# GpSimd starts splitting the second expert's weights after the whole table of tiles instead of after its rows

## The reference

```python
gate_logits = x @ gate_w + gate_b                       # 8 experts
weights, indices = top_k(gate_logits, 2); weights = softmax(weights)
h = einsum('bsd,edh->ebsh', x, w1) + b1                 # w1[e]: 256 x 2048
xh, gh = split(h, 2);  act = silu(gh) * xh
out_e = einsum('ebsf,efd->ebsd', act, w2) + b2          # w2[e]: 1024 x 256
out = sum of the two chosen experts' out_e * weights
x = layernorm(x + out)
```

## Time and profile before

| | us |
|---|---|
| median of 3 runs (lowest, highest) | 1397.85 (1397.28, 1399.97) |
| the profiled execution's own time | 1405.77 |
| its span, first to last instruction | 1403.8 |
| TensorE busy (matmul) | 1253.7, 89% |
| VectorE busy | 1143.5, 81% |
| ScalarE busy | 797.6, 57% |
| GpSimd busy | 786.8, 56% |
| mean granted TensorE clock | 0.959 |

### The profile page before, as it was taken

How to read it: one execution, slowest core, us unless ns; L and a number is a source line. 1 busy time by engine, 2 the same in 40 slices (tenths; PEclk the granted TensorE clock), 3 DMA queues, 4 the chain that set the end, 5 groups by cost and what they waited for, 6 DMA issues and landing times. The chain is left out here.

```text
span 1403.8 us, 40595 instructions
## 1 busy us (share of the span) xinstructions
PE 1253.7 (89%) x13192; PEld 1031.3 (73%) x13193; DVE 1143.5 (81%) x2632; ACT 797.6 (57%) x1863; POOL 786.8 (56%) x743
## 2 busy tenths in 40 slices
PE   4889999999999999899978879999999999999990
PEld 2456666666666676667667768999999999999980
DVE  4889999999999999899976886868677867686666
ACT  5666666666766766676634344544545455445446
POOL 3467676666766787687775340707043706170772
PEclk9899999999999999999966989999999999999995
DMA  6213432334443223321225542231514151412554
GB/s 211 81 35 121 135 100 85 111 109 135 136 136 106 96 62 122 108 87 58 91 112 147 141 118 58 67 117 41 146 45 138 42 146 45 137 43 56 150 144 157
DMA packets 120720, 146.63 MB, mean 104 GB/s; under 512 B 47744, under 2 KB 103552, under 8 KB 120512
## 3 DMA queue, kind: packets, MB, share of 16 engines
q1 hardware_dynamic: 109504, 102.15, 24.1%
q0 software_dynamic: 10848, 42.32, 9.7%
q10 hardware_dynamic: 288, 1.19, 0.2%
HBM read 98.83 MB, written 37.47 MB: 97 GB/s over the span
## 5 line engine op out<-in xcount | busy, mean ns | idle before, releaser
L1111 PE MATMUL pe<-arena 128*128 128x128 f16 x3408 | 218.8, 222 | 26.0 <-issue 19.1
L1111 PEld LDWEIGHTS pe<-arena 128*128 128x128 f16 x3408 | 202.5, 99 | 32.6 <-issue 30.7
L1111 PE MATMUL pa<-arena 128*128 128x128 f16 x3408 | 217.7, 221 | 3.1 <-DVE pm L2315 2.5
L1136 PE MATMUL py<-arena 128*128 (+1 forms) x1704 | 199.4, 274 | 5.5 <-issue 3.3
L1111 PEld LDWEIGHTS pa<-arena 128*128 128x128 f16 x3408 | 200.1, 99 | 3.4 <-DVE pm L2315 2.7
L1572 ACT ACTIVATE arena<-pe,arena 128x128 f32<-128x128 f32 x568 | 161.4, 370 | 68.0 <-PE pe L1111 67.5
L1705 DVE SCALAR_TENSOR_TENSOR arena<-pa,arena 128x511 f32<-128x511 f32 (+2 forms) x240 | 178.7, 745 | 11.7 <-ACT arena L1209 5.6
L1136 PEld LDWEIGHTS py<-arena 128*128 128x128 f16 x1704 | 164.5, 98 | 24.8 <-issue 5.0
L1744 DVE TENSOR_TENSOR_SCAN arena<-arena,pe 128x512 f32<-128x512 f32 x128 | 148.8, 1203 | 3.0 <-issue 1.6
L2557 POOL TENSOR_SCALAR arena<-arena 128x1536 f16<-128x1536 f32 (+2 forms) x35 | 45.3, 1295 | 180.7 <-DVE arena L2363 175.3
L833 PEld LDWEIGHTS py<-arena 128*128 128x128 f32 x1024 | 124.0, 197 | 17.4 <-issue 8.5
(11 more groups left out here) (306 smaller groups left out, 2542.1 us busy)
## 6 DMA issues: line engine op xcount, KB each, us to landing
arena<-step_rows SPq DMA_DIRECT2D x64, 512.0 KB, 5.8
arena<-in_w_exp POOLq DMA_DIRECT2D x32, 768.0 KB, 4.9
arena<-queue SPq DMA_DIRECT2D x74, 129.5 KB
answer<-arena SPq DMA_DIRECT2D x71, 128.0 KB, 1.7
arena<-in_x SPq DMA_DIRECT2D x16, 512.0 KB, 6.1
answer<-zeros SPq DMA_DIRECT2D x10, 512.0 KB, 4.8
arena<-h SPq DMA_DIRECT2D x9, 512.0 KB, 6.2
h<-arena SPq DMA_DIRECT2D x8, 512.0 KB, 3.0
```

The lines of the kernel that those rows point to most:

```text
L1111: ins = pe.matmul(bank[:, f * P:(f + 1) * P], w_split[:, p, hl, d * 2 * FF + col:d * 2 * FF + col + P], x_hl[:, r, x, d * P:(d + 1) * P], ...
L1136: ins = pe.matmul(py[:, 0:D], a[:, b, f, :], part(p, hl, W1N + f * D, D), start=(half == 0 and n == 0), stop=(half == 1 and n == len(passe ...
```

## The change

GpSimd's wait before the split of place 1 becomes the wait for `plan_done`; the separate wait for `plan_done` before the split of place 2 falls away, being the same one. Nothing else is changed: the same instructions, the same loads, the same order on every engine.

```diff
                     pool.wait_ge(w_have, 1)
                 load_weights(e)
                 if e == 1:
-                    pool.wait_ge(rows_done, 1)
-                if e == 2:
                     pool.wait_ge(plan_done, 1)
                 if e >= 2:
                     end_e = pool.value_load(plan_i[0:1, 3 * NJT + NE + e - 2:3 * NJT + NE + e - 1], min_val=0, max_val=NJ)
```

## The result

| | before | changed |
|---|---|---|
| median, us (lowest to highest) | 1399.97 (1397.27 to 1404.04), 7 runs | 1392.64 (1389.72 to 1396.23), 7 runs |
| ratio, 95% interval | | 0.9949 [0.9928, 0.9969] |
| the profiled execution's span | 1403.8 | 1392.5 |

The kernel became faster by 0.5%, 7.3 us between the medians. The forecast was 6.9 us.

A forecast was written before the change was run, and what follows sets the result against it. The prediction took TensorE as the bound, waiting early in the expert stage for VectorE held by GpSimd. -9.4 gained + 2.5 new waits = -6.9 us, so 1397.85 became 1391.0 us, range 1386.0 to 1396.5.

The forecast's parts named there:

- What bounds it, and why VectorE was slow: Expert stage: TensorE bounds; at its start GpSimd's split holds VectorE's SBUF steps, and TensorE loses 11.12 us.
- The gain, 9.4 us: TensorE from product (0,2) to (1,1): 11.12 us lost, less 1.72 kept, gives 9.4 gained.
- The part I kept, 1.72 us of start-up after plan_done: TensorE's idle after plan_done, read as fetching the table's word and new code; 1.72 us expected to stay.
- What comes, 2.5 us of new waits: VectorE held under the later split 1 makes TensorE wait up to (2,2)'s stretch: 2.5 us, bounds 0 and 9.4.
- +4.7 forecast: VectorE's rows_moved, eight chained steps under split 1: seven held, meeting four GpSimd instructions, +4.7 us.
- The held first step of rows_of_pick: VectorE under split 1: the first rows_of_pick meets at most the split's last instruction; no size added.
- Kept at their price: 4.4 us ahead of and in the product of (2,0): TensorE's 2.66 us idle before the product at 841.00 plus 1.7 of lower clock, assumed to stay.
- more gained: Rival, chance 0.13: with third-expert loads later, the stall at product (2,0) goes too; -11.3 us, 1386.6.
- split 2 was released 9.4 us earlier and not 7: Sign of being right in the changed profile: GpSimd's split 2 released 7 us earlier.
- the signs of being wrong: TensorE's VectorE waits between 811 and 835 over 5 us, lower clock past 10 us, or plan_done not 7 us earlier.
- Moved, not removed: Rival, chance 0.13: VectorE's held time under the later split reaches TensorE, up to 9.4 us; 1397 to 1398.
- Slower: Rival, chance 0.08: each held rows_moved step waits out its own GpSimd instruction; +6.2 us, 1404.

The follow-up runs named there:

- e5: Kernel before, with split 1's 15 GpSimd instructions replaced by zero fills that write SBUF and read none; 1390.04 us, ratio 0.9939.
- e0: Kernel before run once more with no edit, as a control; ratio 0.9999 [0.9981, 1.0016].
- e2: Kernel before, with the third expert's weight loads waiting until tile (2,0) is answered, split 1 unmoved; 1396.91 us against 1400.08, ratio 0.9986.
- e7: Kernel before, split 1 still from rows_done, with only VectorE's rows_moved and rows_of_pick steps put two tiles later; ratio 1.000 [0.9983, 1.0018].
- e6: Kernel before, with split 1 started after words, between rows_done and plan_done; 1391.54 us, ratio 0.9945 to the kernel before.
- e3: Changed kernel, with VectorE's rows_moved and rows_of_pick steps put two tiles later, behind split 1; 1389.97 us, ratio 0.9922 to the kernel before.
- e8: The kernel of e3 run again beside the changed kernel; 1390.18 us, ratio 0.9929 to the kernel before.

## Why the prediction was right

The forecast was -6.9 us, with a range of 1386.0 to 1396.5; measured 1392.64, and 7.3 us between the medians. Step by step:

*What bounds it, and why VectorE was slow.* Right. In e5 GpSimd keeps its 15 instructions but reads nothing, and the two-operand steps run free beneath them. The fills are shorter than the split's instructions too, but length alone does not explain it, since a copy and a cast are held beneath the same fills.

*The gain, 9.4 us.* The loss from (0,2) to (1,1) was 11.1, 8.6, 13.6 and 13.3 us in the four traces with split 1 from rows_done and its arithmetic unchanged (before, e0, e2, e7) and 0.7 in the three of the changed kernel: 10.9 us gained on the mean. The part I kept, 1.72 us of start-up after plan_done, was too dear. It is paid where TensorE already stands waiting (1.72 to 1.76 us from plan_done to the next bank in before, e0, e2, e7 and e6); with plan_done early, 0.57 remains. plan_done came at 804.3, 1.7 us ahead of the forecast. Of that, 0.7 is held time in three rows that I had left out (L2227, L2232, L2255), and 1.1 is that VectorE stood further ahead in that execution before the split began. TensorE had no use for it.

*What comes, 2.5 us of new waits.* The mechanism was right and the size low: 2.0, 3.7 and 3.9 us of waits on VectorE in three traces. Shorter delays that the view does not mark come on top. From the product of (1,1) to that of (2,2) the changed kernel lost 4.6, 6.4 and 6.6 us and e3 and e8, which do not wait for VectorE, 1.4 and 1.6. Between the means that is 4.4 us, where the medians of the two pairs give 2.8 and 3.2. Of its terms rows_moved was over-sized, +4.7 forecast and +3.2 measured (4.70 against 1.54), since it met three GpSimd instructions and not four, and only steps with two operands were held; in e6, where five of the eight steps were held, L2266 among them, it cost +3.5. The held first step of rows_of_pick, +1.9 (2.29 against 0.38), I had named and not added, and the last of the new waits (0.95) stands right behind it. e3 and e8 show the two together: without them under the split, the waits are gone.

*Kept at their price: 4.4 us ahead of and in the product of (2,0).* This was the weakest step. I took one profile's stall for the kernel's. At that product nothing was marked in e0 and e2, and 1.74 us in e7, each with matmuls at full pace behind. So it was one execution's and not the kernel's, and the rival "more gained", which took it as a whole, could only come true in the profiled pair (-11.3 us), not in the medians (-7.3). A smaller part of it may be real: the four traces with split 1 from rows_done lost 3.6 us on the mean from (1,1) to (2,2) without any wait on VectorE, and e3 and e8 lost 1.5.

*The sum.* In the traces the stretch up to (2,2) lost 15.3 us on the mean of the four with split 1 from rows_done (17.9, 11.1, 15.3, 16.7) and 6.6 in the three changed: -8.7, to be set beside -7.3, -7.3 and -6.3 between medians; so few traces can't settle the rest. By its parts it is -10.9 up to (1,1), +4.4 from VectorE's lateness behind it and -2.2 from start-up pauses that were shorter. That -9.4 + 2.5 came so near is partly luck, errors that cancel: the gain was 1.5 larger, the waits 1.9 larger, and what I had kept at its price fell by 2.2. Of the signs that I had named, rows_moved was spread over 4.7 us and not 5 to 7, and split 2 was released 9.4 us earlier and not 7; none of the signs of being wrong came true.

*The rivals.* "Moved, not removed" fell: the stretch under the split lost at most 7.3 us where 15 was lost before. It had the right cause, though: VectorE is held for about as long as before (11.5 us against 11.2 to 14.0), and the difference lies in what is queued behind it. "Slower" needed each step of rows_moved to wait out its own GpSimd instruction; in the trace L2261 passed free behind L2260. What stays open is whether the third expert's loads cost TensorE anything in its first pass of the loop. e2's 0.9986 [0.9972, 1.0001] does not settle it, and the traces speak both ways. The four in which these loads begin earliest (before, e0, e7 and e5) each have one pause of 1.7 to 2.7 us there, and the eight others no start-up pause above 0.92; but in e6 a load was in flight at its 0.82.

## What to carry to other kernels

When two engines exclude each other per instruction, ask what is queued behind the loser. The same split left TensorE's settled pace as it was (7.98 us from the product at 884.45 to the next, beneath split 2 of the kernel before) and cost some 10 us beneath a chain of short dependent steps that a third engine waits for. So put long GpSimd work behind such a chain, and put steps that nobody awaits yet behind the GpSimd work: the first edit was worth 7 us by itself, the second 3 more behind the first and nothing measurable alone (e3 and e8 against e7). And take a stall that no semaphore explains from more than one profile before its price enters a sum.

## What the runs showed of the hardware that was not expected

A copy of eight float32 numbers on one partition, 0.16 us when free, took 2.82 us in e6: the length of a held instruction says nothing of its size. Beneath a fill the same copy was held too (1.36 us in e5), while two-operand steps ran free. A tensor_scalar of 7 numbers on 128 partitions, of which no row before showed a hold, took 1.41 us there in place of 0.17.

The stretch from (0,2) to (1,1) took 24.5 to 29.5 us in four executions with split 1 from rows_done, all alike in what runs up to there. Which of VectorE's steps were held differed between them: L2116 behind the words took 1.31 us in the two slowest and 0.42 in the two others. That this makes the difference is argued, not tested. With the split behind the table it took 16.67 to 16.70 in all six traces that start it at plan_done or later. So in this stretch the change took out a spread as well as a mean.
